# Loading the context a second time with channels on the partitions, in a fused fp32 decoder layer on one Trainium2 core

## The chip, the cores and the metric

The kernel is one program on one core of a Trainium2 chip. The core has TensorE (PE, whose weight loads are shown apart as PEld), VectorE (DVE), ScalarE (ACT), GpSimd (POOL) and SyncE (SP, which here issues all DMAs). The metric is the device time of one execution in microseconds (us), lower is better; the times of a kernel are given as the median of several runs.

## The reference

A post-norm decoder layer over 8 batch elements of 256 tokens with 256 channels. `x` is the text, `ctx` the context, both 8 x 256 x 256 in fp32.

```python
x = layernorm(x + attention(x))                 # 16 causal heads of 16 channels
# cross attention with slots: the text rows are the slots
Pn = rmsnorm(ctx, input_norm_w); k = Pn @ Wk.T; v = Pn @ Wv.T
for _ in range(3):
    q = rmsnorm(slots, slot_norm_w) @ Wq.T
    attn = softmax(q @ k.T * 256**-0.5, axis=slots)
    attn = attn / (attn.sum(over context) + 1e-6)
    slots = gru_cell(attn @ v, slots)
x = layernorm(x + slots)
# 16 experts of 64 hidden units, the 4 best gated
x = layernorm(x + experts(x))
```

## The kernel before

Every wide product is done in fp32 precision with three passes of the faster fp32r form: each operand is held as a high part and a low part (tiles whose names end in `_hl`), a product is hi x hi, hi x lo and lo x hi (`split3`, line 430). The high part is a rounding copy on ACT, the low part a subtraction on DVE or POOL.

The program has three stages.

1. Attention (about 25 to 207 us). The unit of work is a quad of heads (four heads of one batch element), 32 in all, each in three thirds, written out in order on every engine. For each quad, `natural` (L1791) computes scores with queries on the partitions only to find the row maxima, DVE takes them (`maxima`, L1243, tile `neg_max`), PE turns them, ACT copies them to `negT`, and SP moves them by DMA into row 96 of the query operand `q_op` (L498 to L504). `turned` (L1817) computes the scores with keys on the partitions from `k_op` and `q_op`: 96 rows of head channels and the 97th that subtracts the maximum. Both tiles have 97 partitions (`K_ROWS + 1`). Work that is not part of the quads (projections, the output projection, the first layer norm) stands beside the thirds, by the table `BESIDE` (L313), in two PSUM banks, 6 and 7, used in turn: a job waits until the reader of the bank's last content is done. The heads' result of a batch element is turned into banks 6 and 7 (`yT`), DVE divides it by the sums (`inverse_sums`, L1256) and writes `y_nat` with two instructions (`heads(n, 0)` and `heads(n, 1)`, L1268); the second of them stands one quad later than the first, behind the maxima of the next quad's first third. The banks are free for the next job, and the transposes of `y_nat` can start, when both are done (`yn_ok`).

2. Cross attention (about 207 to 570 us). Two batch elements are taken as a pair, with three iterations each, so a pair has six units, u = 0 to 5 (`cross`, L2112 on PE). The first three pairs run in a loop, whose pass also prepares the context of the next pair (in units 4 and 5); the fourth pair is written out after it. The context of the first pair is prepared at the end of stage 1 (`first_context`). In a unit PE does `mean_squares` (L1932), `scores` (L1946, 12 matmuls), `scales` (L1955), `inputs` (L2127, 36 matmuls), `state` for the reset gate (12), `totals` (L1964) and `state` for the other two gates (24). `scales` spreads the inverse root mean square `s_rs` of each slot along the partitions: two fp32 matmuls of a broadcast column with the identity `ident`. The result goes by way of ACT (`rs_bc`) to DVE (`soft`, L1344).

   A batch element of the context is prepared like this. SP loads it into `c_in[:, j]` with tokens on the partitions (L569). ACT sums its squares (`context_squares`, L852) in unit 3. PE turns it with four transposes (`context_text`, L1901 to L1904, recorded as L441) into a PSUM bank, for j = 0 at the end of unit 4's `inputs`, for j = 1 behind the context values of j = 0. ACT rounds the bank to the high part of `cT_hl` (`context_text_hi`, L855), DVE subtracts (`context_text_lo`, L1306), and PE multiplies `cT_hl` with the key weights (12 matmuls) and the value weights (36). SP loads the next pair's context once the transposes and the squares of this one are done. The order of the jobs in the PSUM banks is kept by hand in `jobs2` (L376 to L385) and, for the first pair, in `FIRST_BANK`; `bank_free` derives from them what a job waits for. `cT` of j = 1 has bank 1, which the next `scales` uses too.

```python
def context_text(r, j, first=False):
    b = free_bank(r, ("cT", j), first)
    pe.wait_ge(c_arr[j], due(1, r, 2, step=16))
    transpose4(pe, b, lambda t, c: c_in[:, j, t, c * P:(c + 1) * P]).then_inc(cT_mm, 1)
```

3. Experts (about 570 to 672 us), which the change does not touch.

Of the kernel before, what the change touches and what calls it, by code (L numbers as in the profile page):

```python
# [69 lines left out]
def decoder_layer(nc, x, xT, ctx, w_qkv, w_proj, wq, wk, wv, wihT, whhT, eselT, keys, values, cols, lines, out):  # L70
    stack = ExitStack()
    with stack:
# [64 lines left out]
        q_op = sb("q_op", [K_ROWS + 1, 2, 2, H // 2, T], F32R, where=sq_op)  # L137
# [14 lines left out]
        k_op = sb("k_op", [K_ROWS + 1, 2, H // 2, T], F32R, where=s1)  # L152
# [108 lines left out]
        spot_in, spot_ok = sem("spot_in"), sem("spot_ok")  # L261
        set_mm, set_q, set_k = sem("set_mm"), sem("set_q"), sem("set_k")
# [14 lines left out]
        cT_mm, cT_hi, cT_lo = event("cT_mm", 2), event("cT_hi", 2), event("cT_lo", 2)  # L277
# [111 lines left out]
        FIRST_BANK = {("cT", 0): (0, max_ok, 3 * QUADS), ("kT", 0): (1, max_ok, 3 * QUADS),  # L389
                      ("vg", 0): (0, cT_lo, due(2, -1, 3)), ("vg", 1): (1, kT_lo, due(2, -1, 3)),  # L390
                      ("vg", 2): (0, vg_lo, due(6, -1, 7)), ("cT", 1): (1, vg_lo, due(6, -1, 8)),
                      ("kT", 1): (0, vg_lo, due(6, -1, 9)), ("vg", 3): (1, cT_lo, due(2, -1, 4)),
# [61 lines left out]
        def _(sp):  # L454
# [70 lines left out]
            for quad in QUADS_AND_TAIL:  # L525
# [1762 lines left out]
```

## Time and profile before

| | |
|---|---|
| median of 3 runs | 675.24 us (673.99, 675.24, 680.57) |
| the profiled execution, its own time | 674.05 us |
| its span, from the first to the last instruction | 672.3 us |
| mean granted TensorE clock | 0.991 of full speed |
| busy, share of the span | PE 94%, PEld 86%, DVE 74%, ACT 51%, POOL 33% |

Between the span and the execution's own time lie 1.75 us before the first and behind the last instruction. A row of the profile names the line of the program, the engine, the operation, the tile that is written and those that are read ("out<-in"), partitions x elements, the count and the duration; in brackets stands how long the engine had been idle and what it waited for. "L441" is the line of a helper that records all transposes of four blocks; which ones they are is told by the tiles.

### The profile page before, as it was taken

To read this page: it belongs to the slowest core of one execution; us is meant where nothing else is said; L and a number is where in the kernel's file an instruction comes from. 1 tells how busy PE (TensorE), PEld (TensorE's weight loads), DVE (VectorE), ACT (ScalarE), POOL (GpSimd) and SP (SyncE) were. 2 spreads that over 40 slices of the span, in tenths; PEclk is the share of its full clock that TensorE was granted. 3 is DMA by queue.
4 is the path that set the end of the run, shared out by engine and by line. 5 is a ranking of instruction groups with operands and counts; after the bars stand their busy time and mean duration, and the time that the engine had idled before them with its cause. 6 is when DMAs were issued, how large, how long until landed. Compare 5 with 4: busy or idle time off the path is not lost.

```text
span 672.3 us, 14159 instructions
## 1 busy us (share of the span) xinstructions
PE 630.6 (94%) x5144; PEld 577.2 (86%) x5160; DVE 497.9 (74%) x1045; ACT 340.5 (51%) x758; POOL 223.4 (33%) x272
## 2 busy tenths in 40 slices
PE   5889998997989999999999999999999987999996
PEld 5766776776768999999999999999999986999996
DVE  4754666565754888879888798897989978676663
ACT  4434545453674455754556645556466544153350
POOL 9303335233453323213222223123231116062542
PEclk9899999899999999999999999999999998999999
DMA  8635556258300220000000000000000000000000
GB/s 282 204 96 169 148 162 203 77 181 215 78 19 1 75 83 1 16 17 2 0 0 16 16 0 0 0 0 0 0 1 2 0 2 0 17 18 32 0 32 32
DMA packets 24271, 36.96 MB, mean 55 GB/s; under 512 B 2208, under 2 KB 11808, under 8 KB 24224
## 3 DMA queue, kind: packets, MB, share of 16 engines
q1 hardware_dynamic: 24224, 36.34, 18.1%
q8 instruction: 29, 0.48, 0.3%
q14 instruction: 18, 0.15, 0.1%
HBM read 23.10 MB, written 13.11 MB: 54 GB/s over the span
## 4 chain that ended last, share of the span: by engine, by line
PE 56%; issue 13%; DVE 13%; POOL 5%; SPq 5%; DMA 5%; ACT 2%; another core or an unknown queue 1%; DVEq 0%; POOLq 0%; ACTq 0%
PE bank L433 26%; PE bank L2127 11%; PE bank L1946 5%; POOL hid_hl L762 4%; DMA k_rows<-k_hl 3%; PE bank L1955 2%; DMA q_op<-negT 2%; PE bank L441 2%; PE bank L1964 1%; PE bank L1932 1%; PE bank L1846 1%; SPq L503 1%; DVE neg_max L1254 1%; PE bank L1812 1%; PE bank L1827 1%
## 5 line engine op out<-in xcount | busy, mean ns | idle before, releaser
L433 PE MATMUL bank<-slots_hl,whhT_hl 128*128 128x256 f32 x864 | 113.8, 284 | 0.0
L433 PEld LDWEIGHTS bank<-slots_hl,whhT_hl 128*128 128x128 f32 x864 | 106.2, 188 | 2.5 <-ACT gate_z L1065 1.0
L2127 PE MATMUL bank<-attn_hl,vg_hl 128*128 128x256 f32 x864 | 107.0, 282 | 0.0
L1254 DVE TENSOR_REDUCE neg_max<-bank 128x2 f32<-128x512 f32 (+1 forms) x96 | 65.5, 690 | 53.4 <-PE bank L1814 37.4
L2127 PEld LDWEIGHTS bank<-attn_hl,vg_hl 128*128 128x128 f32 x864 | 102.6, 189 | 0.2 <-POOL attn_hl L672 0.2
L831 ACT ACTIVATE pT<-bank 128x512 f32<-128x512 f32 x96 | 56.9, 598 | 53.2 <-PE bank L1827 37.7
L643 POOL TENSOR_SCALAR_AFFINE_SELECT pT<-pT 128x512 f32<-128x512 f32 x64 | 40.5, 636 | 116.3 <-ACT pT L831 116.2
L657 POOL TENSOR_TENSOR sq<-sq 128x256 f32<-128x256 f32 x24 | 18.1, 753 | 172.8 <-ACT sq L1050 130.8
L762 POOL TENSOR_TENSOR hid_hl<-hid,hid_hl 128x512 fp32r<-128x512 f32 x32 | 41.1, 1303 | 32.7 <-ACT hid_hl L776 32.4
L433 PE MATMUL bank<-x2T_hl,keys_hl 128*128 128x256 f32 x384 | 50.3, 285 | 0.3 <-ACT hid L1139 0.3
L433 PE MATMUL bank<-values_hl,hid_hl 128*128 128x256 f32 x384 | 49.1, 286 | 0.3 <-DVE x L1530 0.3
L433 PEld LDWEIGHTS bank<-x2T_hl,keys_hl 128*128 128x128 f32 x384 | 47.3, 191 | 1.1 <-ACT hid L1139 0.9
L433 PEld LDWEIGHTS bank<-values_hl,hid_hl 128*128 128x128 f32 x384 | 47.2, 193 | 0.7 <-DVE x L1530 0.5
L1364 DVE RECIPROCAL inv_tot<-tot 128x256 f32<-128x256 f32 x24 | 42.1, 1753 | 0.8
L1946 PE MATMUL bank<-slots_hl,kT_hl 128*128 128x256 f32 x288 | 39.3, 286 | 0.0
L433 PE MATMUL bank<-v_w_hl,cT_hl 128*128 128x256 f32 x288 | 37.2, 285 | 0.0
L433 PE MATMUL bank<-xT_hl,wqkv_hl 128*128 128x512 f32 (+1 forms) x120 | 28.7, 391 | 8.6 <-DVE xT_hl L1192 6.5
L1827 PE MATMUL bank<-q_op,k_op 97*128 97x512 f32 x64 | 32.9, 519 | 4.1 <-DMA q_op<-negT 4.1
L433 PEld LDWEIGHTS bank<-v_w_hl,cT_hl 128*128 128x128 f32 x288 | 35.2, 188 | 0.8 <-issue 0.6
L1946 PEld LDWEIGHTS bank<-slots_hl,kT_hl 128*128 128x128 f32 x288 | 35.2, 189 | 0.0
L776 ACT ACTIVATE attn_hl<-attn 128x512 fp32r<-128x512 f32 x24 | 15.1, 631 | 34.8 <-DVE attn L1370 34.8
L1055 ACT ACTIVATE gate_r<-bank,brz_col 128x256 f32<-128x256 f32 x48 | 20.2, 472 | 24.2 <-PE bank L2127 24.2
(209 smaller groups left out, 1332.9 us busy)
## 6 DMA issues: line engine op xcount, KB each, us to landing
q_rows<-q_hl SPq DMA_DIRECT2D x21, 256.0 KB
k_rows<-k_hl SPq DMA_DIRECT2D x21, 256.0 KB
q_op<-q_rows SPq DMA_DIRECT2D x28, 192.0 KB, 3.2
k_op<-k_rows SPq DMA_DIRECT2D x14, 384.0 KB, 4.8
x_in<-in_x_dram SPq DMA_DIRECT2D x8, 256.0 KB, 6.5
c_in<-in_ctx_dram SPq DMA_DIRECT2D x8, 256.0 KB, 4.7
out_dram<-y_out SPq DMA_DIRECT2D x8, 256.0 KB, 2.1
xT_in<-in_xT_dram SPq DMA_DIRECT2D x3, 512.0 KB, 5.7
```

Source lines behind the costliest of these rows:

```text
L433: mm = pe.matmul(dst, left(a), right(b), start=first and n == 0, stop=last and n == 2, skip_group_check=True)
L643: pool.affine_select(out=tile, in_=tile, compare_op=ALU.is_ge, fill=0.0, base=0, pattern=[[0, 4], [1, P]], channel_multiplier=-1).then_inc ...
L657: pool.tensor_tensor(sq[:, 0, :], sq[:, 0, :], sq[:, 1, :], ALU.add).then_inc(sq_sum, 1)
L762: pool.tensor_tensor(hid_hl[:, j, LO, 2 * g:2 * g + 2, :], hid[:, n % HIDDEN, :, :], f32(hid_hl[:, j, HI, 2 * g:2 * g + 2, :]), ALU.subtra ...
L776: return act.activation(dst, src, ACT.Copy, **kw)
L831: act.activation(dst, bank[2 + (3 * quad + third) % 2][:, :].rearrange("p (h n) -> p h n", h=4 if third == 2 else 2), ACT.Exp).then_inc(ex ...
L1055: r = act.activation(gate_r[:, c, :], halves(4)[:, c, :], ACT.Tanh, scale=0.5, bias=brz_col[:, c:c + 1])
L1254: dve.tensor_reduce(dst, src, AX.X, ALU.max, negate=True).then_inc(max_ok, 1)
L1364: dve.reciprocal(inv_tot[:, :], tot[:, :]).then_inc(it_ok, 1)
L1827: mm = pe.matmul(halves(b), k_op[:, n % 2, pair_of(quad, third), 0:P], q_op[:, n % 2, :, pair_of(quad, third), :], start=True, stop=True)
L1946: mm = pe.matmul(halves(b)[:, t, :], kT_hl[:, j, k_part, c, t * P:(t + 1) * P], slots_hl[:, j, s_part, c, :], start=n + t + c == 0, stop=n ...
L2127: mm = pe.matmul(halves(b)[:, m, :], vg_hl[:, j, v_part, 3 * t + r, q:q + P], attn_hl[:, j, at_part, t, :], start=n == 2 and a + m + t == ...
```

## The change

- The input of the context is passed twice, as it was and with its two inner axes exchanged on the host (`ctxT`). SP loads a batch element as before for the squares, and when these are done (`c_sq`) it loads `ctxT` into the same `c_in[:, j]` (`turned_context`). The four transposes per batch element on PE (`context_text`) are gone with their semaphore and their place in the bank orders; ACT and DVE read `c_in` instead of a bank. SP's wait for the next pair's load is now on `cT_lo`, the low part of this one.
- `k_op` and `q_op` have 128 partitions instead of 97; the added rows hold ones and zeros. `turned` multiplies over 128 rows. POOL's memsets cover the added rows, with two more of them for `q_op`'s first batch element, and a semaphore `rows_ok`.
- `scales` uses the transpose form of the matmul in place of the plain fp32 form, twice per unit as before.
- In stage 1 DVE writes the second half of `y_nat` right behind the first, ahead of the next quad's first maxima.

```diff
-        q_op = sb("q_op", [K_ROWS + 1, 2, 2, H // 2, T], F32R, where=sq_op)
+        q_op = sb("q_op", [P, 2, 2, H // 2, T], F32R, where=sq_op)
...
-        k_op = sb("k_op", [K_ROWS + 1, 2, H // 2, T], F32R, where=s1)
+        k_op = sb("k_op", [P, 2, H // 2, T], F32R, where=s1)
...
-            cT, kT, *vg = ((0, 1, 3, 2, 0), (1, 0, 3, 6, 7))[j]
-            jobs = [(("cT", j), cT, cT_lo, 2, 2 + j + 1), (("kT", j), kT, kT_lo, 2, 2 + j + 1)]
+            kT, *vg = ((1, 3, 2, 0), (0, 3, 6, 7))[j]
+            jobs = [(("kT", j), kT, kT_lo, 2, 2 + j + 1)]
...
+            def turned_context(i, j):
+
+                sp.wait_ge(c_sq, due(2, i, j + 1))
+                sp.sem_inc(passed, 1)
+                sp.dma_start(c_in[:, j, :, :], rows(ctxT[i * 2 + j, :, :], NC)).then_inc(cT_arr[j], 16)
...
+                if quad in (QUADS - 6, QUADS - 5):
+                    turned_context(0, quad - (QUADS - 6))
...
-                    sp.wait_ge(cT_mm, due(2, i, j + 1, back=1))
-                    sp.sem_inc(passed, 1)
-                    sp.wait_ge(c_sq, due(2, i, j + 1, back=1))
+                    sp.wait_ge(cT_lo, due(2, i, j + 1, back=1))
                     sp.sem_inc(passed, 1)
                     sp.dma_start(c_in[:, j, :, :], ctx[i * 2 + j, :, :].rearrange("(t p) d -> p t d", p=P)).then_inc(c_arr[j], 16)
+                for j in range(2):
+                    turned_context(i, j)
...
-                pool.memset(f32(k_op[K_ROWS:K_ROWS + 1, batch, :, :]), 1.0).then_inc(consts, 1)
+                pool.memset(f32(k_op[K_ROWS:, batch, :, :]), 1.0).then_inc(consts, 1)
...
+            for e in range(2):
+                pool.memset(f32(q_op[K_ROWS:, 0, e, :, :]), 0.0).then_inc(rows_ok, 1)
+            pool.wait_ge(rows_ok, 2)
...
             def context_text_hi(r, j, first=False):
-                act.wait_ge(cT_mm, due(2, r, 2 + j + 1))
+                act.wait_ge(cT_arr[j], due(1, r, 2, step=16))
                 act.wait_ge(vg_mm, due(6, r, 6 + 3 * j))
-                copy(cT_hl[:, HI, :, :], halves(context_bank(("cT", j), first))).then_inc(cT_hi, 1)
+                copy(cT_hl[:, HI, :, :], c_in[:, j, :, :]).then_inc(cT_hi, 1)
...
                 dve.wait_ge(cT_hi, due(2, r, 2 + j + 1))
-                sub_hi(cT_hl[:, LO, :, :], halves(context_bank(("cT", j), first)), cT_hl[:, HI, :, :]).then_inc(cT_lo, 1)
+                sub_hi(cT_hl[:, LO, :, :], c_in[:, j, :, :], cT_hl[:, HI, :, :]).then_inc(cT_lo, 1)
...
                         inverse_sums(2 * period - 1)
                         heads(2 * period - 1, 0)
-                    elif key == (2, 0) and 0 <= 2 * period - 1 < B:
                         heads(2 * period - 1, 1)
...
                 for t in range(NT):
-                    mm = pe.matmul(bank[b][:, t * P:(t + 1) * P], s_rs[:, j, t:t + 1].to_broadcast([P, P]), ident[:, :],
-                                   start=True, stop=True)
+                    mm = pe.transpose(bank[b][:, t * P:(t + 1) * P], s_rs[:, j, t:t + 1].to_broadcast([P, P]), ident[:, :])
...
-                    if u == 4 and not last:
-                        context_text(i, 0)
...
                         context_values(i, 0)
-                        context_text(i, 1)
```

The order on DVE in stage 1, where the heads' result of batch element 1 is divided (`inv` are the inverse sums, `neg_max` the maxima, `y_nat` the divided result). Before:

```order
L1254 TENSOR_REDUCE neg_max<-bank 128x2 [waits neg_mm,n_mm] x2
L1261 RECIPROCAL inv<-bank 128x16 [waits yn_ok,yT_mm]
L1261 RECIPROCAL inv<-bank 128x16
L1268 TENSOR_TENSOR y_nat<-bank,inv 128x256 [waits y_mm,inv_ok]
L1254 TENSOR_REDUCE neg_max<-bank 128x2x2 [waits neg_mm,n_mm]
L1268 TENSOR_TENSOR y_nat<-bank,inv 128x256 [waits y_mm,inv_ok]
L1254 TENSOR_REDUCE neg_max<-bank 128x2 [waits neg_mm,n_mm]
```

And now:

```order
L1267 TENSOR_REDUCE neg_max<-bank 128x2 [waits neg_mm,n_mm] x2
L1274 RECIPROCAL inv<-bank 128x16 [waits yn_ok,yT_mm]
L1274 RECIPROCAL inv<-bank 128x16
L1281 TENSOR_TENSOR y_nat<-bank,inv 128x256 [waits y_mm,inv_ok] x2
L1267 TENSOR_REDUCE neg_max<-bank 128x2x2 [waits neg_mm,n_mm]
L1267 TENSOR_REDUCE neg_max<-bank 128x2 [waits neg_mm,n_mm]
```

The second `y_nat` has moved from behind one `neg_max` to ahead of it; the same holds for the other batch elements.

The order on PE in the loop of stage 2, from the values of context 0 to the inputs of unit 5. Before:

```order
L433 MATMUL bank<-v_w_hl,cT_hl 128x256 [waits ms_ok]
L433 MATMUL bank<-v_w_hl,cT_hl 128x256 x11
L441 MATMUL bank<-ident,c_in 128x128 [waits c_arr1,kT_lo]
L441 MATMUL bank<-ident,c_in 128x128 x3
L1946 MATMUL bank<-slots_hl,kT_hl 128x256 [waits kT_lo,sl_hi,vg_lo]
L1946 MATMUL bank<-slots_hl,kT_hl 128x256 x7
L1946 MATMUL bank<-slots_hl,kT_hl 128x256 [waits sl_lo]
L1946 MATMUL bank<-slots_hl,kT_hl 128x256 x3
L1898 REGISTER_ALU
L1955 MATMUL bank<-ident,s_rs 128x128 [waits rs_ok,cT_lo]
L1955 MATMUL bank<-ident,s_rs 128x128
L2127 MATMUL bank<-attn_hl,vg_hl 128x256 [waits vg_lo,at_hi]
```

And now:

```order
L434 MATMUL bank<-v_w_hl,cT_hl 128x256 [waits ms_ok]
L434 MATMUL bank<-v_w_hl,cT_hl 128x256 x11
L1953 MATMUL bank<-slots_hl,kT_hl 128x256 [waits kT_lo,sl_hi,vg_lo]
L1953 MATMUL bank<-slots_hl,kT_hl 128x256 x7
L1953 MATMUL bank<-slots_hl,kT_hl 128x256 [waits sl_lo]
L1953 MATMUL bank<-slots_hl,kT_hl 128x256 x3
L1962 MATMUL bank<-ident,s_rs 128x128 [waits rs_ok,kT_lo]
L1962 MATMUL bank<-ident,s_rs 128x128
L2130 MATMUL bank<-attn_hl,vg_hl 128x256 [waits vg_lo,at_hi]
```

The four transposes of `c_in` are gone, and `scales` waits for `kT_lo` of context 0 instead of `cT_lo` of context 1. In unit 4 the other four are gone in the same way.

## Rows read from the trace of the kernel before

**Rows 1.** The page: the chain that ended last, by engine.

```profile
PE 56%; issue 13%; DVE 13%; POOL 5%; SPq 5%; DMA 5%; ACT 2%; another core or an unknown queue 1%; DVEq 0%; POOLq 0%; ACTq 0%
```

**Rows 2.** Windows (us, busy and count per engine): a loop pass, part of the last pair.

```profile
321.00:404.00 83.00, 82.35 (x678) 80.21 (x677) 72.17 (x134) 47.12 (x119) 22.50 (x24) 1.00 0.02 6
487.00:540.00 53.00, 50.74 (x413) 48.94 (x413) 48.12 (x83) 30.73 (x71) 11.65 (x13) 1.00 0.01 1
```

**Rows 3.** Timeline of PE, second pass of the loop, units 4 to 5: start, duration.

```profile
365.32 0.60 PE L441 MATMUL bank<-ident,c_in 128*128 128x128 f32 x4
365.68 1.66 PE L433 MATMUL bank<-slots_hl,whhT_hl 128*128 128x256 f32 x12
...
376.94 1.62 PE L1946 MATMUL bank<-slots_hl,kT_hl 128*128 128x256 f32 x12
378.91 0.71 PE L1955 MATMUL bank<-ident,s_rs 128*128 128x128 f32 x4 [0.35 <-DVE cT_hl L1192]
379.38 4.35 PE L2127 MATMUL bank<-attn_hl,vg_hl 128*128 128x256 f32 x36
```

**Rows 4.** Timeline of DVE there: low parts of the values, the next softmax.

```profile
375.64 1.52 DVE L1323 SCALAR_TENSOR_TENSOR vg_hl<-bank,c_rs,vg_hl 128x512 fp32r<-128x512 f32 x3
...
380.23 0.88 DVE L1344 SCALAR_TENSOR_TENSOR attn<-bank,c_now,rs_bc 128x256 f32<-128x256 f32 x2 [1.30 <-ACT rs_bc L776]
```

**Rows 5.** Timeline of a plain unit in the loop, around scales.

```profile
347.87 0.16 DVE L1335 TENSOR_SCALAR s_ms<-bank 128x2 f32<-128x2 f32 x1 [0.22 <-PE bank L1932]
...
348.96 0.63 ACT L776 ACTIVATE attn_hl<-attn 128x512 fp32r<-128x512 f32 x1 [0.58 <-DVE attn L1370]
349.23 0.68 PE L1955 MATMUL bank<-ident,s_rs 128*128 128x128 f32 x4
...
349.67 0.60 PE L2127 MATMUL bank<-attn_hl,vg_hl 128*128 128x256 f32 x3
```

**Rows 6.** Timeline in attention, around y_nat.

```profile
96.61 0.69 DVE L1254 TENSOR_REDUCE neg_max<-bank 128x4 f32<-128x512 f32 x1 [0.42 <-PE bank L1807]
...
97.21 0.41 DVE L1268 TENSOR_TENSOR y_nat<-bank,inv 128x256 f32<-128x256 f32 x1
97.68 0.42 PEld L433 LDWEIGHTS bank<-wqkv_hl,xT_hl 128*128 128x128 f32 x3 [0.95 <-DVE y_nat L1268]
```

**Rows 7.** Tile y_nat, who waited for it (us in total, times).

```profile
  PEld bank L433: 3.7, 4
```

**Rows 8.** The chain that ended last, in attention: start, duration.

```profile
80.98 1.39 PE bank L433 x6
...
85.09 0.32 SPq L491
...
108.60 0.50 PE bank L1827
...
119.95 2.65 PE bank L433 x6
...
203.19 0.23 PE bank L1827
```

**Rows 9.** Timeline of ACT where the first context is turned.

```profile
193.47 0.60 ACT L776 ACTIVATE cT_hl<-bank 128x512 fp32r<-128x512 f32 x1 [0.76 <-PE bank L441]
```

**Rows 10.** ACT in the loop: the last square, the rounding copy; landing of c_in.

```profile
359.14 0.40 ACT L852 ACTIVATE junk<-c_in 128x256 f32<-128x256 f32 x1
...
367.07 0.59 ACT L776 ACTIVATE cT_hl<-bank 128x512 fp32r<-128x512 f32 x1
...
DMA to landing us min/median/max: 2.6/4.7/8.4
```

**Rows 11.** Timeline of POOL at the start.

```profile
6.58 3.54 POOL L615 MEMSET q_op<- 97x2048 f32 x2
...
23.05 2.72 POOL L693 TENSOR_TENSOR wproj_hl<-st_proj,wproj_hl 128x512 fp32r<-128x512 f32 x1 [6.52 <-ACT eselT_hl L776]
```

**Rows 12.** Windows: 2 us of attention; PEclk is the number after POOL's count.

```profile
120.00:122.00 2.00, 2.00 (x6) 1.56 (x7) 0.00 (x0) 0.00 (x0) 0.00 (x0) 0.58 0.32 78
```

More of the change, by code:

```diff
@@ L66, in after, with decoder_layer @@
         engine.wait_ge(signal, count)
-def decoder_layer(nc, x, xT, ctx, w_qkv, w_proj, wq, wk, wv, wihT, whhT, eselT, keys, values, cols, lines, out):
+def decoder_layer(nc, x, xT, ctx, ctxT, w_qkv, w_proj, wq, wk, wv, wihT, whhT, eselT, keys, values, cols, lines, out):
     stack = ExitStack()
@@ L261, in decoder_layer @@
         spot_in, spot_ok = sem("spot_in"), sem("spot_ok")
+        rows_ok = sem("rows_ok")
         set_mm, set_q, set_k = sem("set_mm"), sem("set_q"), sem("set_k")
@@ L276, in decoder_layer @@
         c_sq, c_mean, c_rstd, c_kept = event("c_sq", 2), event("c_mean", 2), event("c_rstd", 2), event("c_kept", 1)
-        cT_mm, cT_hi, cT_lo = event("cT_mm", 2), event("cT_hi", 2), event("cT_lo", 2)
+        cT_arr = [event(f"cT_arr{j}", 1, 16) for j in range(2)]
+        cT_hi, cT_lo = event("cT_hi", 2), event("cT_lo", 2)
         kT_mm, kT_hi, kT_lo = event("kT_mm", 2), event("kT_hi", 2), event("kT_lo", 2)
@@ L379, in decoder_layer @@
             jobs2 += (front(u + 1) if 0 < u < UNITS - 1 else front(u + 1)[1:]) + back(u)
-            jobs2 += context(0)[:1] if u == 4 else []
             jobs2 += mid(u + 1) if u + 1 < UNITS else []
-            jobs2 += front(UNITS)[:1] + context(0)[1:] + context(1)[:1] if u == 4 else []
-        jobs2 += context(1)[1:2] + mid(UNITS)[:1] + context(1)[2:] + [(("uT", 0), 2, x2_ok, 2, 1)] + front(UNITS + 1)[:1]
+            jobs2 += front(UNITS)[:1] + context(0) if u == 4 else []
+        jobs2 += context(1)[:1] + mid(UNITS)[:1] + context(1)[1:] + [(("uT", 0), 2, x2_ok, 2, 1)] + front(UNITS + 1)[:1]
         jobs2 += mid(UNITS)[1:] + [(("uT", 1), 0, x2_ok, 2, 2)]
         BANK2 = {job[0]: job[1] for job in jobs2}
[L389 to L392, printed above, removed]
+        FIRST_BANK = {("kT", 0): (1, max_ok, 3 * QUADS),
+                      ("vg", 0): (0, max_ok, 3 * QUADS), ("vg", 1): (1, kT_lo, due(2, -1, 3)),
+                      ("vg", 2): (0, vg_lo, due(6, -1, 7)),
+                      ("kT", 1): (0, vg_lo, due(6, -1, 9)), ("vg", 3): (1, vg_lo, due(6, -1, 8)),
                       ("vg", 4): (1, vg_lo, due(6, -1, 10)), ("vg", 5): (0, kT_lo, due(2, -1, 4)),
@@ L501, in maxima @@
                 sp.wait_ge(neg_ok, hh + 1)
+                after(sp, rows_ok, 2 if hh == 0 else 0)
                 for e in range(2):
@@ L1496, in _ @@
                         heads(2 * period, 0)
-                    elif key == (6, 0) and 0 <= 2 * period < B:
                         heads(2 * period, 1)
@@ L1824, in turned @@
                     pe.wait_ge(neg_in[hh % 2], 32 * (hh // 2 + 1))
+                    after(pe, rows_ok, 2 if hh == 0 else 0)
                 after(pe, exp_ok, fill - 1)
@@ L1899, in free_bank @@
                 return b
-            def context_text(r, j, first=False):
-                b = free_bank(r, ("cT", j), first)
-                pe.wait_ge(c_arr[j], due(1, r, 2, step=16))
-                transpose4(pe, b, lambda t, c: c_in[:, j, t, c * P:(c + 1) * P]).then_inc(cT_mm, 1)
             def context_keys(r, j, first=False):
@@ L1980, in first_context @@
             def first_context(quad):
-                if quad == QUADS - 4:
-                    context_text(-1, 0, True)
-                elif quad == QUADS - 3:
+                if quad == QUADS - 3:
                     context_keys(-1, 0, True)
```

4 lines of the change are left out of this document (2 added, 2 removed).

## The prediction

> **What bounds the kernel now.** I read the page first: the table says that PE is busy for 94% of the span, and the chain that ended last lies on PE for 56%, on DVE for 13% and in "issue" for 13%, with SP's queue and DMAs for 5% each [rows 1]. So PE is the engine to relieve, but not everywhere. The windows say where: in a pass of the cross-attention loop PE works 82.35 of 83 us and DVE 72.17, so a microsecond taken from PE can be a microsecond of time; in the last pair, which DVE fills with extra work on the experts' weights, PE works 50.74 of 53 us and DVE 48.12 [rows 2]. The third view is the timeline of single units: who is late at each step. There the reader should look at start times, because durations of matmuls overlap: four transposes last "0.60" in the row, but the next matmul starts 0.36 us after them (365.32 to 365.68), so they cost PE 0.36 us, 0.09 each [rows 3].
>
> **The transposes that go.** There are eight batch elements, two outside the loop and six in it. In a pass of the loop the eight transposes cost 2 x 0.36 = 0.72 us. A third gain stands behind them: `scales` of the next unit uses the bank of the second context and waited 0.35 us for DVE to finish `cT_hl` [rows 3]; now it waits for `kT_lo`, which is done some 2 us earlier. That would be 1.07 us per pass, but something else is late next. The `scores` before it write bank 3, whose last reader is the low part of the first values. These are three DVE instructions from 375.64 that last 1.52 us together with overlap [rows 4]; the first ends at about 376.35. Without transposes PE would be there at 376.94 - 0.72 = 376.22, so it waits to about 376.45. The `scores` start 0.49 us earlier instead of 0.72. They take PE some 1.44 us, so `scales` starts at 377.89 instead of 378.91: 1.02 us earlier. DVE and ACT make these low parts from work that does not depend on the transposes, so I let them stay in place.
>
> **scales as transposes.** A unit has two of these matmuls, but four records [rows 3, 5]: the plain fp32 form goes through the array twice. The transposes of `c_in` have one record each, and the spacing is 0.09 us in both. So PE saves two records, 0.18 us, per unit, in 24 units 4.3 us if all of it counted. It does not. In a plain unit `attn_hl` ends at 348.96 + 0.63 = 349.59 and `inputs` starts at 349.67, 0.44 after `scales` began, where four free records take 0.36: `inputs` waits for ACT, not for `scales` [rows 5]. That chain begins at the matmuls before `scores`, for whose result DVE waited 0.22 us [rows 5], and does not contain `scales`. So in plain units the 0.18 becomes waiting of PE. It counts where `attn_hl` is long done and DVE waits: DVE sat idle 1.30 us for `rs_bc` in unit 5 [rows 4]. There I take the whole 0.18 in each pass, and once more at the end of attention. In the first units of a pass DVE is the late one and may start its softmax somewhat sooner; bounds 0 and 0.18 us per pass, I take 0.07, nearer to the plain unit's zero, 0.2 in three passes. In the last pair I take nothing: 48.12 of 53 us are DVE's own [rows 2], and its low parts stand between `attn_hl` and the softmax.
>
> Together a pass: 1.02 + 0.18 = 1.20 us, which DVE can follow because its own chain restarts at that softmax. Three passes: 3.6 us. From both sides: 0 if DVE takes all, 3 x (1.07 + 0.18) = 3.75 if bank 3 is no limit.
>
> **The second half of y_nat.** This is the part that the name of the change does not mention. Banks 6 and 7 are freed, and the transposes of `y_nat` may start, after both halves. The second half stood behind a maximum of 0.69 us that had itself to wait 0.42 us for PE [rows 6]. The 0.41 us instruction fits into that hole, so the maximum is hardly later and PE's projection starts when PE is ready: 0.95 us in this place [rows 6]. Four projections waited like this, 3.7 us of idle weight loading in all [rows 7], and two turns of `y_nat` some 0.45 us each. Not all of it is on the path. From 85.09 the chain runs through SP's queue and its DMAs to the matmul at 108.60 [rows 8], and the same pattern stands between 131 and 156 us; the waits that lie inside those stretches (at 97.68 and near 143) only lengthen PE's next wait for the maxima's DMA. What is left: 0.95 at 75.8, 0.5 at 119.95 (there the first half was late too), and 2 x 0.45 at 167 and 183: 2.35 us. The bounds are 0 and 3.7 + 0.9 = 4.6.
>
> **The end of attention.** ACT waited 0.76 us for the first context's transposes, and PE's next transposes wait for ACT behind it [rows 9]. With `c_in` already in place that wait goes; the copy of `a_sb` comes 0.65 us sooner, which I take, between 0 and 0.76. For the second context ACT is itself late (it rounds the values first), so I take 0. The `scales` there gives the 0.18 from above.
>
> **What costs.** Full rows: a 512-column matmul over 97 rows takes 0.23 us on the chain, six of 128 rows take 1.39, also 0.23 each [rows 8]. So 0. The second load: 256 KB on an idle queue. The last square ends at about 359.5, the rounding copy begins at 367.07 [rows 10]; with the median landing of 4.7 us it is there at 364.3, with the longest, 8.4, at 368, and ACT would be 0.9 late. Near 182 us SP issues the same loads between two moves of maxima; an issue occupies SP some 0.4 us, and it waits only for squares that are done by then. I take 0. The memsets: two of 2048 elements took 3.54 us, and POOL then sat idle for 6.52 us before `wproj_hl` [rows 11]; two more fit in. Cover gone, this would cost nothing before `wproj_hl` is needed at quad 0. The low part now has both operands in SBUF; `attn_hl` is such a subtraction and takes 0.69 us, as from the bank. 0.
>
> **The sum.** 3.6 + 0.2 + 0.65 + 0.18 + 2.35 = 6.98 us, against the profiled execution's own 674.05: 667.1. The median of the runs shown is 1.2 us above that execution; I go half way and say 667.6 us.
>
> **A rule that speaks against it.** The trace shows what a lower clock costs: at 120 to 122 us the granted clock was 0.58, mostly its level of 1.2 GHz [rows 12], and six matmuls took 2.65 us instead of 1.39, 1.26 more [rows 8]. Ahead of it PE had waited for `y_nat` and DMAs. The Trainium skill ("TensorE: Matmul & The Clock Gate", Part 4) says that transposes do not count as PE being busy in the way matmuls do; by that rule each unit would look a little less busy to the clock, and 32 removed transposes would help. In the loop, which has both kinds, the granted clock was 1.00 [rows 2], so the trace shows no such loss so far.
>
> **Rivals.**
> - *DVE takes the loop's gain* (17%). PE's earlier `scores` and `inputs` end in waits for DVE, and the loop's 3.6 + 0.2 us vanish: 667.6 + 3.8 = 671.4. For it: DVE works 72.17 of 83 us and its backlog fills the first units. Against it: the 1.30 us of idle time [rows 4] right where the gain arises.
> - *SP's chain takes attention's gain* (13%). The 2.35 us end in waits for maxima: 667.6 + 2.35 = 670.
> - *More waits vanish* (14%). The y_nat part gives 4 us, the slow stretch at 120 us goes (1.3) and the halved `scales` counts in half of the 18 loop units (1.6): 667.6 - 1.7 - 1.3 - 1.6 = 663.
> - *The clock falls in the units* (3%): slower. The mechanism is PE's activity around `scales`, fewer matmuls and one more wait for ACT in each of 24 units, so that the clock drops to its lower level for some 2.6 us. Each such fall costs 1.26 us [rows 8]; 24 of them 30 us, so 667.6 + 30 = 698. It decides from 12 falls on, where 15 us exceed the 7 gained by more than 1%.
> - *The load is late* (3%): ACT waits some 0.9 us for the turned context in each pass, 667.6 + 2.7 = 670.3; the transposes would then have been replaced by a wait.
>
> **How the numbers follow.** The forecast has 50%, from 665 to 669.5. A measurement of this kernel tells about 1% from no change; 1% of 675.24 is 6.75, so faster by over 1% is below 668.5. Of the forecast's 50% I put 38 there, and the 14 of the third rival: 52%. Within 1%: the other 12, 17, 13 and 3: 45%. Slower: 3%. The range for 8 in 10 goes from 663.5, with most of the favourable rival, to 672, with both rivals that eat a part.
>
> **What would show it.** Right: no row of `c_in` on PE; `scales` with 48 records instead of 96; a pass of the loop 1.2 us shorter; no wait of PE for `cT_hl`; in plain units the same length and a wait of PE ahead of `inputs`; no wait of weight loads for `y_nat` at 75, 119, 167 and 183 us, and longer waits for the maxima's DMA near 108 and 155. Wrong: a pass as long as before, with new idle time on PE behind DVE; ACT waiting for a DMA ahead of `cT_hl`; plain units shorter too; a granted clock below 1.00 in the loop.

## The result and the profile after

The changed kernel took 670.46 us (median of 9 runs, 665.06 to 672.39) against 675.23 us (9 runs, 672.03 to 680.57): ratio 0.9917, 95% interval 0.9889 to 0.9944. The forecast was 667.6 us with a range of 663.5 to 672.0. The profiled execution was the fastest of the nine: its own time is 665.06 us, its span 663.4 us at a mean granted clock of 0.993, 8.9 us below the span before. So two differences have to be explained: 8.9 us between two profiled executions, and 4.8 us between two medians.

The page's chain by engine; "SPq" and "DMA" are SP's queue and the transfers.

```profile
PE 47%; DVE 16%; issue 14%; SPq 8%; DMA 6%; POOL 5%; ACT 4%; DVEq 0%; POOLq 0%; ACTq 0%
```

Against [rows 1], PE has lost 9 points; SP's queue and DVE have 3 more each. The groups of instructions of the page have no `c_in` on PE any more, and the tile `s_rs` has 48 records on L1962 where L1955 had 96. The windows of a loop pass and of the last pair, as [rows 2]:

```profile
321.00:404.00 83.00, 82.05 (x671) 78.91 (x669) 73.19 (x136) 47.19 (x120) 22.51 (x24) 1.00 0.04 13
487.00:540.00 53.00, 50.18 (x411) 47.54 (x411) 47.18 (x87) 30.10 (x72) 10.43 (x11) 1.00 0.01 1
```

PE's rows still cover 99% of a pass, but durations of matmuls overlap and hide short waits, so where work off PE is time has to be read from start times. The granted clock stays 1.00. PE in the second pass, from the values of context 0 to the inputs of unit 5 (the first view is the whole timeline there, with PEld, the second PE's alone; start, duration):

```profile
370.52 0.65 PEld L1953 LDWEIGHTS bank<-slots_hl,kT_hl 128*128 128x128 f32 x5 [0.34 <-DVE vg_hl L1336]
```

```profile
365.96 4.43 PE L434 MATMUL bank<-v_w_hl,cT_hl 128*128 128x256 f32 x36
370.52 1.68 PE L1953 MATMUL bank<-slots_hl,kT_hl 128*128 128x256 f32 x12
372.04 0.38 PE L1962 MATMUL bank<-ident,s_rs 128*128 128x128 f32 x2
372.18 4.00 PE L2130 MATMUL bank<-attn_hl,vg_hl 128*128 128x256 f32 x33
```

This is the place of [rows 3]. The transposes are gone, `scores` now wait 0.34 us for DVE's `vg_hl`, which is the limit of bank 3 that the prediction expected, and `scales` have no wait. Counted from the `scales` of unit 4 (360.56 before, 354.66 after), `scores` start 0.52 us earlier, `scales` 0.97 and `inputs` 1.30. DVE and ACT there, as [rows 4] and [rows 10]:

```profile
373.03 0.88 DVE L1357 SCALAR_TENSOR_TENSOR attn<-bank,c_now,rs_bc 128x256 f32<-128x256 f32 x2 [0.44 <-ACT rs_bc L789]
```

```profile
353.24 0.40 ACT L865 ACTIVATE junk<-c_in 128x256 f32<-128x256 f32 x1
...
361.15 0.62 ACT L789 ACTIVATE cT_hl<-c_in 128x512 fp32r<-128x512 f32 x1
```

```profile
DMA to landing us min/median/max: 2.5/2.8/8.6
```

DVE's wait of 1.30 us fell to 0.44. The last square ends at 353.64 and the copy starts 7.5 us later. The landing times above are those of both loads of `c_in`; the eight second loads alone took 2.7 to 3.4 us, so the second load is hidden. ACT has no wait for a DMA in the loop. The plain unit, as [rows 5], and the waits of weight loads for `y_nat` and the maxima's DMAs in attention (60 to 212 us: total, times, longest), as [rows 7]:

```profile
342.01 0.16 DVE L1348 TENSOR_SCALAR s_ms<-bank 128x2 f32<-128x2 f32 x1 [0.23 <-PE bank L1939]
...
343.11 0.63 ACT L789 ACTIVATE attn_hl<-attn 128x512 fp32r<-128x512 f32 x1 [0.59 <-DVE attn L1383]
343.38 0.40 PE L1962 MATMUL bank<-ident,s_rs 128*128 128x128 f32 x2
...
343.79 4.17 PEld L2130 LDWEIGHTS bank<-attn_hl,vg_hl 128*128 128x128 f32 x36 [0.25 <-ACT attn_hl L789]
```

```profile
PEld bank L1839 <- DMA q_op<-negT: 6.7, 5, 2.3
PEld bank L1816 <- DMA k_op<-k_rows: 2.7, 3, 1.4
...
PEld bank L442 <- DVE y_nat L1281: 1.0, 1, 1.0
...
PEld bank L434 <- DVE y_nat L1281: 0.2, 1, 0.2
```

Before, the projections waited 3.7 us for `y_nat` [rows 7], and `q_op` and `k_op` cost 5.0 and 2.1 us in the same view; now it is 0.2, 6.7 and 2.7. The transposes of `y_nat` (L442) waited 0.9 us for it before, in two places, and 1.0 now, in one. The fate of [rows 6], the row pair that this part rested on:

```profile
95.92 0.76 DVE L1281 TENSOR_TENSOR y_nat<-bank,inv 128x256 f32<-128x256 f32 x2
...
96.91 1.50 PEld L434 LDWEIGHTS bank<-wqkv_hl,xT_hl 128*128 128x128 f32 x12
```

Both halves run back to back and the matmuls behind them have no wait. At the end of attention, as [rows 9]:

```profile
189.21 0.61 ACT L789 ACTIVATE cT_hl<-c_in 128x512 fp32r<-128x512 f32 x1
...
208.02 0.58 ACT L789 ACTIVATE a_sb<-bank 128x512 f32<-128x512 f32 x1
```

PE there before:

```profile
194.61 1.09 PE L1876 MATMUL bank<-ident,a_sb 128*128 128x128 f32 x8 [0.71 <-ACT a_sb L776]
...
200.28 0.51 PE L1831 MATMUL bank<-q_op,k_op 97*128 97x256 f32 x2 [1.03 <-ACT pT L831]
...
212.93 1.09 PE L1876 MATMUL bank<-ident,a_sb 128*128 128x128 f32 x8 [0.48 <-ACT a_sb L776]
```

And now:

```profile
190.35 1.09 PE L1888 MATMUL bank<-ident,a_sb 128*128 128x128 f32 x8 [0.25 <-ACT a_sb L789]
...
195.14 0.63 PE L442 MATMUL bank<-ident,y_nat 128*128 128x128 f32 x4 [0.60 <-DVE y_nat L1281]
...
196.01 0.51 PE L1843 MATMUL bank<-q_op,k_op 128*128 128x256 f32 x2 [0.24 <-ACT pT L844]
...
208.66 1.09 PE L1888 MATMUL bank<-ident,a_sb 128*128 128x128 f32 x8 [0.95 <-ACT a_sb L789]
```

For the first context PE's wait for `a_sb` fell from 0.71 to 0.25 us. For the second it rose from 0.48 to 0.95: what PE saved on the transposes it waited for ACT. The windows at [rows 12] show where another part of the 8.9 us is from:

```profile
118.00:120.00 2.00, 1.70 (x8) 0.86 (x8) 1.97 (x6) 0.76 (x2) 0.24 (x1) 1.00 1.01 246
120.00:122.00 2.00, 2.00 (x14) 1.69 (x14) 0.50 (x2) 0.94 (x3) 0.00 (x0) 1.00 0.43 112
122.00:124.00 2.00, 2.00 (x28) 1.45 (x27) 2.00 (x4) 1.78 (x4) 1.19 (x2) 1.00 0.00 1
```

A slow stretch is one at the lower level of the clock, as in [rows 12]; this execution had none in attention. The marks of the two traces then read: the first `scales` of the cross stage start 4.22 us earlier (219.05 to 214.83), the last ones 8.74 us (527.76 to 519.02), the end 8.9 us. So 4.2 us are from attention and 4.5 from the cross stage; what follows keeps its length within 0.24 us.

### The profile page after: what moved, and what is told of

Same layout as the page of the kernel before. It is cut to its first block, busy times and chain, and to the rows that moved or that the text cites. A ratio compares the mean times of both kernels' runs of the same rounds, so it can differ in the third digit from the quotient of the medians.

```text
span 663.4 us, 14034 instructions
## 1 busy us (share of the span) xinstructions
PE 621.5 (94%) x5080; PEld 564.9 (85%) x5080; DVE 497.8 (75%) x1045; ACT 339.3 (51%) x758; POOL 227.6 (34%) x274
## 4 chain that ended last, share of the span: by engine, by line
PE 47%; DVE 16%; issue 14%; SPq 8%; DMA 6%; POOL 5%; ACT 4%; DVEq 0%; POOLq 0%; ACTq 0%
PE bank L434 20%; PE bank L2130 9%; PE bank L1953 4%; POOL hid_hl L775 4%; DMA k_rows<-k_hl 3%; SPq L505 2%; DMA q_op<-negT 2%; SPq L492 2%; PE bank L1939 1%; PE bank L1858 1%; DVE gate_r L1617 1%; PE bank L442 1%; PE bank L1970 1%; SPq L483 1%; DVE inv_tot L1377 1%
## 5 line engine op out<-in xcount | busy, mean ns | idle before, releaser
L2130 PEld LDWEIGHTS bank<-attn_hl,vg_hl 128*128 128x128 f32 x864 | 100.9, 188 | 4.3 <-ACT attn_hl L789 3.9
L1839 PE MATMUL bank<-q_op,k_op 128*128 128x512 f32 x64 | 32.4, 512 | 5.2 <-DMA q_op<-negT 5.2
```

Source lines behind the costliest of these rows:

```text
L1839: mm = pe.matmul(halves(b), k_op[:, n % 2, pair_of(quad, third), 0:P], q_op[:, n % 2, :, pair_of(quad, third), :], start=True, stop=True)
L2130: mm = pe.matmul(halves(b)[:, m, :], vg_hl[:, j, v_part, 3 * t + r, q:q + P], attn_hl[:, j, at_part, t, :], start=n == 2 and a + m + t == ...
```

## The experiments

Each kernel was timed beside runs of the kernel before, and its ratio is to these. The figures from traces are collected in a table behind them.

**Control.** The kernel before, unchanged.

> The kernel before, unchanged, to see the granted clock of several of its runs. The changed kernel's profiled run had a span of 663.4 us at a mean clock of 0.993, 8.9 us under the span before at 0.991, but its eight other runs had 666.6 to 670.6 at 0.983 to 0.988, and the medians differ by only 4.8 us. Theory A (the clock wanders alike in both kernels, the profiled run of after was a lucky one): the runs of before lie around a mean clock of 0.985 to 0.990 too, with spans near 673. Theory B (the changed kernel meets slow stretches more often and gives about 4 us back): the runs of before lie at 0.990 or higher, so clearly above those of after.

677.39 us (12 runs), ratio 1.0031 (1.0005 to 1.0056): so 0.3% can come from nothing, and since this interval leaves out 1, the intervals of the ratios are somewhat too narrow. Its runs lie at a mean clock of 0.983 to 0.991 (mean 0.988), and the 91 runs of before beside all experiments have the same mean (0.9883, median 675.95 us). Theory A: the clock wanders alike in both.

**Only y_nat moved.**

```diff
                         heads(2 * period - 1, 0)
-                    elif key == (2, 0) and 0 <= 2 * period - 1 < B:
                         heads(2 * period - 1, 1)
...
                         heads(2 * period, 0)
-                    elif key == (6, 0) and 0 <= 2 * period < B:
                         heads(2 * period, 1)
```

> Only the second half of y_nat is moved. Theory A (my term of 2.35 us, and as much of it as is not absorbed by SP's chain): the first scales of the cross stage, at 219.05 us before, starts 2.35 us earlier, and 1.3 more if the slow stretch at 120 us is gone; everything after it runs with periods as before (82.8 us per pass). Theory B (SP's chain of maxima takes all of it): first scales within 0.5 us of 219.05, with longer waits for the DMA of the maxima. Ratio under A 0.9965, under B 1.000.

672.3 us, ratio 0.9957 (0.9938 to 0.9977). The first `scales` stand at 220.06 against 219.05 and 222.19 in two traces of one and the same kernel before, so a single mark does not decide. The ratio favours theory A (a gain of 1.6 to 4.2 us by its interval), but the 0.43% lie little above the 0.31% that the control gave for nothing. What decides are the stretches between reciprocals in all traces, below.

**Only the context's second load.**

```diff
-                act.wait_ge(cT_mm, due(2, r, 2 + j + 1))
+                act.wait_ge(cT_arr[j], due(1, r, 2, step=16))
...
-                copy(cT_hl[:, HI, :, :], halves(context_bank(("cT", j), first))).then_inc(cT_hi, 1)
+                copy(cT_hl[:, HI, :, :], c_in[:, j, :, :]).then_inc(cT_hi, 1)
...
-                    if u == 4 and not last:
-                        context_text(i, 0)
...
-                        context_text(i, 1)
```

SP's loads, waits and the plan of banks are those of the changed kernel.

> Only the context's transposes are replaced by the second load. Theory A (my working): each pass is 1.02 us shorter (82.8 to 81.8), all of it between the scales of unit 4 and of unit 5; the end of attention gives 0.65 us at the first scales. Ratio 0.9945. Theory B (the second load or its waits cost something): ACT waits for a DMA ahead of cT_hl or SP's moves near 182 us come late, the pass gets less than 0.5 us shorter and attention's end nothing; ratio 0.999 or more.

672.69 us, ratio 0.9946 (0.9921 to 0.9971). Passes of 81.66 and 81.68 us against 82.64 before (the mean of the four kernels in the table with both parts as before): 0.97 us each, theory A. Of it 0.87 lie between the `scales` of units 4 and 5, where the expectation had all of it, and 0.10 behind them. ACT has no wait for a DMA ahead of `cT_hl`.

**Only full rows.**

```diff
-        q_op = sb("q_op", [K_ROWS + 1, 2, 2, H // 2, T], F32R, where=sq_op)
+        q_op = sb("q_op", [P, 2, 2, H // 2, T], F32R, where=sq_op)
...
-        k_op = sb("k_op", [K_ROWS + 1, 2, H // 2, T], F32R, where=s1)
+        k_op = sb("k_op", [P, 2, H // 2, T], F32R, where=s1)
```

The memsets and waits that go with them are in too.

> Only the operands' rows go from 97 to 128. Theory A (my working: a matmul takes the same time with 97 or 128 rows, the fills are hidden): start and loop as before, ratio 1.000, mean clock as in the kernel before. Theory B (full rows let the clock stay up in attention, which is where the slow stretch at 120 us went): no granted clock below 1.00 between 107 and 154 us, mean clock higher by 0.002 or more than before, 1.3 us or more faster.

675.85 us, ratio 1.0015 (0.9993 to 1.0036), a mean clock of 0.9886 over its runs, two slow stretches in attention (from 31 and from 157 us). Theory A.

**The changed kernel again.**

> The changed kernel once more, all four parts. So far each alone: y_nat 672.3, context 672.69, rows 675.85 against 675.66 us before. Theory A (the parts add up, and the profiled 665.06 us was a lucky run): median 669 to 670.5, first scales of the cross stage between 215 and 220 us, passes of 81.38 us as in the first profile. Theory B (together they reach what the profile showed): median 666 to 667, first scales near 215 us again.

668.0 us (8 runs, 665.94 to 673.89), ratio 0.9899 (0.9864 to 0.9933), below the band that theory A named; the profiled span was 669.9 us at a clock of 0.987. Its first `scales` stand at 221.42, above theory A's 220 too, 6.6 us later than in the first profile of the same kernel; from there to the last `scales` it is 304.19 us in both traces. So the first profile was a lucky one, in attention alone, and theory B falls. Theory A is what is left, with both of its bands missed by one microsecond or more. Windows of this trace:

```profile
108.00:110.00 2.00, 0.00 (x0) 0.00 (x0) 1.31 (x6) 0.00 (x0) 0.59 (x1) 1.00 0.55 169
110.00:112.00 2.00, 1.37 (x5) 1.01 (x6) 0.00 (x0) 0.54 (x2) 0.00 (x0) 0.55 0.48 150
112.00:114.00 2.00, 2.00 (x13) 2.00 (x12) 0.00 (x0) 0.31 (x2) 0.00 (x0) 0.59 0.82 215
166.00:168.00 2.00, 0.59 (x5) 0.59 (x6) 0.00 (x0) 0.00 (x0) 0.00 (x0) 1.00 1.09 215
168.00:170.00 2.00, 2.00 (x9) 1.38 (x10) 0.90 (x2) 0.85 (x2) 0.00 (x0) 0.56 0.76 124
170.00:172.00 2.00, 2.00 (x14) 1.77 (x16) 0.75 (x2) 1.19 (x2) 0.63 (x1) 0.59 0.28 82
```

Two stretches of the lower level, each with 2 x (0.45 + 0.41) = 1.7 us lost (1.7 likewise in the second), so 3.4 of the 6.6 us. Ahead of each PE had stood for a DMA, 3.12 and 2.74 us; in the view of waits above `q_op` and `k_op` cost 12.0 us here and 9.4 in the first profile, which is much of the rest.

**The change without its y_nat part** (the two lines of the second experiment are back).

> The changed kernel with the second half of y_nat back behind the maximum. Theory A (y_nat worth 2.35 us as forecast, 3.4 us measured alone): 2.3 to 3.4 us slower than the changed kernel of the same call, four waits for y_nat of 3.7 us in all are back, loop passes 81.38 us. Theory B (the gain of y_nat in company is taken by SP's chain): within 1 us of the changed kernel.

670.0 us (9 runs), 2.0 us above the 668.0 us of the changed kernel, timed beside it, and 0.7 above the median of all its 17 runs. That is in the band of neither theory and inconclusive, since the ratios' intervals (0.9880 to 0.9939 and 0.9864 to 0.9933) overlap. The waits for `y_nat` are back in its trace (3.1 us in four places ahead of projections, 1.9 ahead of its transposes), and its passes are 81.33 and 81.35 us, as expected.

**Only scales as transposes.**

```diff
-                    mm = pe.matmul(bank[b][:, t * P:(t + 1) * P], s_rs[:, j, t:t + 1].to_broadcast([P, P]), ident[:, :],
-                                   start=True, stop=True)
+                    mm = pe.transpose(bank[b][:, t * P:(t + 1) * P], s_rs[:, j, t:t + 1].to_broadcast([P, P]), ident[:, :])
```

> The kernel before with only scales as transposes. Theory A (my working: in plain units PE then waits for ACT, so 0.18 us counts once per pass, some 0.25 with the first units): passes of 82.5 us against 82.75, plain units still 11.33 us, ratio 0.9988. Theory B (halved scales count in every unit): plain units 11.15, passes 1.1 us shorter, ratio 0.9935.

676.29 us, ratio 0.9998 (0.9965 to 1.0032): what it gives is too small for a comparison of times. The trace tells it: passes of 82.26 and 82.30 us (82.64 before), plain units 11.31. PE where unit 5 starts:

```profile
381.21 0.43 PE L1955 MATMUL bank<-ident,s_rs 128*128 128x128 f32 x2 [0.31 <-DVE cT_hl L1192]
381.39 1.85 PE L2126 MATMUL bank<-attn_hl,vg_hl 128*128 128x256 f32 x14
```

`inputs` follow 0.18 us behind `scales`, where it was 0.47 in [rows 3] (378.91 to 379.38). Theory A, with more in unit 5 than I gave it: 0.36 us per pass instead of 0.25.

**The change with scales as matmuls.**

```diff
-                    mm = pe.transpose(bank[b][:, t * P:(t + 1) * P], s_rs[:, j, t:t + 1].to_broadcast([P, P]), ident[:, :])
+                    mm = pe.matmul(bank[b][:, t * P:(t + 1) * P], s_rs[:, j, t:t + 1].to_broadcast([P, P]), ident[:, :],
+                                   start=True, stop=True)
```

> The changed kernel with scales as plain matmuls again, four records instead of two. The context alone gave passes of 81.75 us, the whole change 81.38. Theory A: passes 81.7 us and plain units 11.33, so the difference lies in the first unit after unit 5 alone; 1.1 us slower in three passes. Theory B: the difference is spread over the plain units.

669.25 us (10 runs), 1.25 above the changed kernel timed beside it, within the noise of both. Passes of 81.67 and 81.73 us against 81.36: 0.34 us. Of it 0.22 lie in the interval behind unit 5 and 0.03 in each plain unit. Theory A, though not all of it is in one interval.

**Scales four times.**

```diff
+                    for _ in range(4):
-                    mm = pe.transpose(bank[b][:, t * P:(t + 1) * P], s_rs[:, j, t:t + 1].to_broadcast([P, P]), ident[:, :])
+                        mm = pe.transpose(bank[b][:, t * P:(t + 1) * P], s_rs[:, j, t:t + 1].to_broadcast([P, P]), ident[:, :])
```

> The changed kernel with each transpose of scales issued four times, eight records per unit instead of two, 0.54 us more work on TensorE (6 at 0.09). In the changed kernel's plain units PE waits 0.25 us for ACT's attn_hl behind scales. Theory A (that wait is slack behind which scales hides, which is why halving it gave nothing there): plain units grow by 0.54 - 0.25 = 0.29 us, from 11.31 to 11.60, and units outside by the whole 0.54; a pass has 3 plain ones and 3 others, so 81.37 becomes 83.9. Theory B (scales is on the path in every unit, and the gain of halving it went elsewhere): plain units grow by 0.54 to 11.85. Theory C (PE has far more slack there): no growth.

677.65 us (10 runs), passes of 83.70 and 83.59 us. A plain unit:

```profile
350.36 1.66 PE L1953 MATMUL bank<-slots_hl,kT_hl 128*128 128x256 f32 x12
352.05 1.06 PE L1963 MATMUL bank<-ident,s_rs 128*128 128x128 f32 x8
352.87 0.36 PE L2131 MATMUL bank<-attn_hl,vg_hl 128*128 128x256 f32 x1
```

Eight records hold PE 0.79 us or a little more (0.79 in unit 5, where nothing else holds `inputs` back; two hold it 0.14 there). In a plain unit `inputs` follow 0.41 us behind `scales` with two records, and 0.82 here. These 0.41 more are what the unit grew by, 11.31 to 11.70. Theory A in kind; the growth was 0.39 and not 0.29, because six more records cost 0.65 us and not 0.54. In a plain unit `scales` cost nothing up to about 0.4 us and everything above. Outside the plain units the expectation of 0.54 us each did not hold: the interval behind unit 5 grew by 0.68 us, that of unit 5 by 0.37, the one behind these two by 0.06, so the pass grew by 2.3 us and not by 2.5.

**Mean squares earlier.** A try at a faster kernel: the matmuls for which DVE waits 0.23 us in a plain unit go two matmuls ahead of the end of the state's last group.

```diff
-                            mm = split3(pe, halves(b)[:, m, :], lambda a: whhT_hl[:, a, c, cols],
-                                        lambda a: slots_hl[:, j, a, c, :], m == 0 and c == 0, False)
+                            for k, (a_w, a_s) in enumerate(PASSES):
+                                if squares and name == "hn" and m == 1 and c == 1 and k == 1:
+                                    mean_squares(i, u + 1)
+                                mm = pe.matmul(halves(b)[:, m, :], whhT_hl[:, a_w, c, cols], slots_hl[:, j, a_s, c, :],
+                                               start=m == 0 and c == 0 and k == 0, stop=False, skip_group_check=True)
```

The call at the head of the next unit is gone for it.

> The changed kernel with the four mean-square matmuls of units 2 to 5 issued two matmuls before the end of the state's last group, instead of behind it. In a plain unit DVE ends inv_tot at 341.78, waits 0.23 us for these matmuls, and everything up to ACT's attn_hl, for which PE waits 0.25 us ahead of inputs, stands behind that. Theory A (this is the chain that sets the plain unit): the wait of DVE goes, attn_hl comes 0.2 us earlier, plain units last 11.1 us instead of 11.31, in the last pair nothing (DVE-bound): 0.2 in 3 to 4 units of 3 passes, 2 us in all, median 666. Theory B (the plain unit is set elsewhere, by the gates' chain on DVE and ACT): units stay at 11.3 and PE's wait moves to another place. Theory C (PE stops 0.1 to 0.2 us ahead of the matmuls, for POOL's squares, and that takes the gain back): units within 0.05 us of 11.31, with a wait of PE for sq.

669.74 us, ratio 0.9904 (0.9869 to 0.9938); passes of 81.33 and 81.41 us, plain units 11.32. The whole timeline of one:

```profile
355.31 1.75 DVE L1377 RECIPROCAL inv_tot<-tot 128x256 f32<-128x256 f32 x1
...
357.18 0.16 DVE L1348 TENSOR_SCALAR s_ms<-bank 128x2 f32<-128x2 f32 x1
...
357.25 0.68 DVE L1382 TENSOR_TENSOR attn<-attn,inv_tot 128x256 f32<-128x256 f32 x1
...
357.86 0.47 DVE L1383 SCALAR_TENSOR_TENSOR attn<-attn,s_inv,inv_tot 128x256 f32<-128x256 f32 x1
...
359.05 1.59 PEld L2133 LDWEIGHTS bank<-attn_hl,vg_hl 128*128 128x128 f32 x13 [0.21 <-ACT attn_hl L789]
```

DVE's wait is gone and nothing came of it. `s_ms` starts 1.87 us after `inv_tot` instead of 1.98, but the next instruction lasts 0.68 instead of 0.58 us, and the one behind it starts 2.55 after `inv_tot` instead of 2.57; PE still waits 0.21 us for ACT. The wait stood beside another limit of DVE's own chain behind the reciprocal. Theory A falls. What theory C named is there as well: PE stops for some 0.2 us ahead of the squares, whose matmuls start at 356.56 where POOL's `sq` ends at 356.42. But the gain was lost on DVE, and `inputs` still wait for ACT and not for PE, so this stop is not shown to hold the unit. B fits best, though which step of the gates' chain sets the 11.31 us was not tried.

**The change with 97 rows.** The diff of full rows, backwards.

> The changed kernel with the operands at 97 rows again and without the additional memsets. Alone the full rows gave 675.85 us against 675.66. Theory A (they cost and give nothing in company either): the median within 1 us of the changed kernel's 668.0 to 670.5, loop passes 81.35 us, and as many slow stretches of the clock between 28 and 212 us as in the changed kernel's traces (none and two so far, four traces of variants with one to three). Theory B (full rows keep PE's clock up in attention, so that the profiled run of the change had no slow stretch there): more than two slow stretches and 1.7 us for each, median above 671.

671.56 us (6 runs, 666.97 to 673.36), ratio 0.9897 (0.9843 to 0.9950). The median lies 0.06 us above the band of theory A (667.0 to 671.5) and in that of theory B, but its ratio is the changed kernel's, and its trace has passes of 81.32 and 81.40 us and two slow stretches, not more: theory A by the trace.

The traces together. "First" is the start of the first `scales`, "slow" the number of stretches of the lower clock between 28 and 212 us, "first, less" the start without 1.7 us for each; a pass is the mean of two, the unit 5 interval runs from the `scales` of unit 4 to those of unit 5, the next one from there to the following unit.

| kernel | first | slow | first, less | pass | plain unit | unit 5 | next |
|---|---|---|---|---|---|---|---|
| before | 219.05 | 1 | 217.35 | 82.79 | 11.34 | 18.35 | 18.15 |
| before again | 222.19 | 2 | 218.79 | 82.52 | 11.30 | 18.21 | 18.17 |
| rows alone | 220.86 | 2 | 217.46 | 82.64 | 11.34 | 18.20 | 18.14 |
| scales alone | 222.22 | 2 | 218.82 | 82.28 | 11.31 | 18.20 | 17.85 |
| context alone | 221.98 | 2 | 218.58 | 81.67 | 11.31 | 17.38 | 18.06 |
| after, no y_nat | 222.52 | 3 | 217.42 | 81.34 | 11.31 | 17.33 | 17.83 |
| y_nat alone | 220.06 | 2 | 216.66 | 82.62 | 11.31 | 18.25 | 18.17 |
| after | 214.83 | 0 | 214.83 | 81.38 | 11.31 | 17.38 | 17.83 |
| after again | 221.42 | 2 | 218.02 | 81.35 | 11.31 | 17.33 | 17.82 |
| after, scales matmul | 219.29 | 2 | 215.89 | 81.70 | 11.34 | 17.35 | 18.05 |
| after, scales x4 | 220.16 | 3 | 215.06 | 83.65 | 11.70 | 17.72 | 18.51 |
| squares early | 218.86 | 3 | 213.76 | 81.37 | 11.32 | 17.29 | 17.84 |
| after, 97 rows | 220.93 | 2 | 217.53 | 81.36 | 11.31 | 17.34 | 17.82 |

The six kernels with `y_nat` as before have a mean "first, less" of 218.07, the seven with it moved 215.96: 2.1 us, with a standard deviation of 0.7 and 1.5 us between traces of a group, so it is known to some 0.7. The groups differ in more than `y_nat`: the context's second load, worth 0.7 us at the end of attention, is in two of the six and in six of the seven, which makes 0.4 of the 2.1; and the moved group happens to reach its first reciprocal 0.7 us later, before any `y_nat` is written. With both taken out it is 2.4 us. Cut at the reciprocals of the batch elements (DVE, `inv`), with the same 1.7 us taken off, the six stretches of attention change by these means (from the first `inv` to the second, and so on; the last runs from the sixth to the first `scales` and holds the context's gain too): -1.01, +0.13, -0.59, -0.33, -0.21, -0.80 us. In the first stretch all seven lie at 20.85 to 21.36 us and all six at 21.81 to 22.55, in the third at 21.09 to 21.16 and 21.61 to 21.78: there the gain is shown. In the second, fourth and fifth the groups overlap widely, and their means say little.

## Why the prediction was right

All 17 runs of the changed kernel have a median of 669.27 us and a mean of 669.39; the 91 runs of before 675.95 and 676.23. That is 6.7 and 6.8 us, where the sum forecast 6.98. The first comparison's 4.8 was low and the profiled 8.9 high, as the second set of runs shows with 8.6 against its own neighbours (668.0 to 676.57). The 670.46 us lie inside the range, but outside the 665 to 669.5 us that had 50%, and under 1% from no change, which had 45%; the terms below are what bears the forecast out, and that their sum comes so near is in part luck, since the term for `y_nat` is known to some 0.7 us only.

- *Transposes in the loop.* Forecast 1.02 us per pass, with bank 3 as the next limit; measured 0.97 with the context alone, and the limit stands in the trace (0.34 us for `vg_hl`). Right in mechanism and size.
- *Halved scales.* Forecast 0 in plain units and 0.18 + 0.07 in the rest of a pass; measured 0.03 at most in a plain unit and 0.34 to 0.36 in a pass. The term mis-sized is the 0.18 for unit 5: two records there hold PE 0.14 us and four 0.36, so 0.22, and alone it is 0.30. I had divided 0.36 by four and called 0.09 the spacing. In unit 5 the starts of the records are 0.11 us apart in both forms, and the next matmul starts 0.03 behind the last one, so one record less is 0.11.
- *A pass together.* Forecast 1.20, measured 82.64 - 81.36 = 1.28. DVE did not take it back, so the first rival is out. The whole cross stage up to the last `scales` got 4.1 us shorter against the mean of four kernels with both parts as before (308.3 to 304.19), forecast 3.8.
- *y_nat.* Forecast 2.35 us; measured 2.1 in the traces as they are and 2.4 with the two corrections above, each to some 0.7, and 1.6 to 4.2 by the runs of it alone. By place: 0.95 forecast and 1.01 measured between the first two reciprocals, 0.5 and 0.59 around 119.95; 0 and -0.13 (loss) around 97.68, 0 and 0.33 around 143, 0.45 and 0.21 around 167, which are within the scatter; and 0.45 at 183, where the two `y_nat` pairs without other differences give 0.42 (before again to y_nat alone, 37.96 to 37.54) and 0.40 to 0.43 (after, no y_nat to after and after again, 37.20 to 36.77 and 36.80). That SP's chain takes the whole is refuted. It seems to take part: the waits for its DMAs in the view above rose from 7.1 to 9.4 us, and from 8.2 to 9.8 in the means of the six and the seven traces, but they run from 7.1 to 9.1 and from 7.1 to 12.0.
- *End of attention.* Forecast 0.65, with 0 for the second context and its `scales` at 0.18. From the sixth reciprocal to the first `scales` the context gives 0.68 alone (37.96 to 37.28) and 0.74 in company (37.54 with y_nat alone to 36.80). Right for a partly different reason: PE gained 0.85 us by 191.61 us, of which 0.46 is the shorter wait for `a_sb` and the rest the transposes that are gone, for which I had counted nothing here. The new wait of 0.60 us for `y_nat` took nothing back, because PE's next wait, for `pT`, fell from 1.03 to 0.24. Some 0.1 us was lost behind 211.38, where PE's last transposes of `y_nat` stand behind DVE's wait for POOL's `std` (2.53 us, 2.38 before). The second context gave nothing, as said. The 0.18 of `scales` does not come there (37.95 alone) but once two units later, between the third and fourth `scales` (11.52 to 11.34).
- *Costs at nothing.* Full rows, the load, the memsets: right. POOL's idle time ahead of `wproj_hl` was 6.52 us [rows 11] and is 3.25 now; the cover held. Without the full rows the changed kernel is not clearly slower or faster (six runs).
- *Wrong reasoning without a cost.* I read [rows 5] as a chain that begins at the matmuls for which DVE waited 0.22 us. With these matmuls 0.2 us earlier the unit kept its length, so they do not set it.
- *The rival with the slow stretch.* I gave 1.3 us to a change in which the stretch at 120 us goes. It is not the kernel's: the same kernel has one or two of them at other places (120; 110 and 168). The slower rival, a clock that falls in the units, has nothing for it: 1.00 in every loop, and a mean clock of 0.9877 over the runs of after against 0.9883.

The Trainium skill ("TensorE: Matmul & The Clock Gate", Part 4) had transposes count less as busy time for the clock. No run here shows it either way: with 80 fewer records of `scales` and `c_in` or with eight of them per unit the clock in the loop stayed at 1.00.

What stays open: with the slow stretches taken off, attention still differs by up to 3.2 us between traces of one kernel (214.83 and 218.02). The waits for DMAs differ along with it; what makes them differ was not tried.

## What to carry to other kernels

Price an edit where PE is the late one: 0.22 us of work off PE counted in full behind unit 5 and hardly at all in the plain units, where ACT's result came 0.41 us after `scales` began. Before counting on an idle interval, ask what would hold the next instruction if it went: the 0.23 us that DVE waited bought nothing. With a stage that wanders by some microseconds from run to run, compare intervals inside the stages of several traces, and let no single profiled execution stand for the median.

## What was not expected of the hardware

The slow stretches in attention are all of one size: a loss of 1.7 us each, none to three of them in an execution, starting near 31, 68, 110, 120, 157 to 160 or 168 us. Two records of `scales` as transposes hold the next matmul back by 0.14 us, four by 0.36 and eight by 0.79: each record starts 0.11 us behind the one ahead, and the matmul behind the last one is recorded only 0.03 us later, so 0.14 / 2 is no price of a record.
